# Addressing the expert weights in bytes, loading all tiles' numbers at once, and making three low halves after the first turned rows

## The chip, the cores and the metric

The kernel runs on one core of a Trainium2 chip. The time is that of the device, in microseconds, for one execution. The kernel before was timed in three runs; each kernel was also run once under the hardware profiler, and all rows below come from that execution.

## What is computed

The reference is two blocks of gated cross attention and feed-forward over x of 8 x 100 rows of 256 numbers, in float32:

```python
x = x + tanh(g_xattn[0]) * xattn0(layernorm(x), ctx)
x = x + tanh(g_ffn[0])   * ffn0(layernorm(x))
x = x + tanh(g_xattn[1]) * xattn1(layernorm(x), ctx, ctx)
x = x + tanh(g_ffn[1])   * moe(layernorm(x))
# moe: scores = softmax(x @ gate_w + gate_b), the two best of 8 experts
#      h = relu(x @ w1[e] + b1[e]);  y = h @ w2[e] + b2[e];  out = sum over the two of score * y
```

The change touches only the last line, the mixture of experts: 800 rows, each to two of E = 8 experts with hidden width DF = 1024.

## The kernel before, in words

Everything ahead of the last stage (layernorms, first block, second attention) fills the span up to about 540 us. While the second attention runs, the expert weights are brought in by POOL's queue and split in two fp16 halves, a high one (ACT) and a low one (DVE, raw value times 16 minus the high half, L1446). All eight experts stay in the on-chip tile WE, per partition `[E, 4, 2048]` fp16: m = 0, 1 are high and low of w1, m = 2, 3 of w2. One half step n = 1 to 16 makes one matrix of one expert, from expert 7 down to expert 0; LATE = 10, and steps 10 to 16 are made in the last stage by `act_step` (L1824) and `dve_step` (L1992). Semaphore s_wlo counts low halves.

The last stage sorts the 1600 (row, expert) pairs into NS = 20 tiles of 128 slots, each tile of one expert; tiles go from expert 7 to expert 0. DVE makes from the counts, for each tile, the expert number `em` and the count of low halves that must be there, `ew` = 16 - 2 e (L2087, L2088). Then the tiles are worked, and five engines run programs of their own that meet by semaphores:

- POOL (L1798 to L1819): `gather(a)` is an indirect DMA of tile a's 128 rows into one of three buffers `xg`. Three gathers go out first; then for each a it waits until tile a is turned, gathers a + 3, waits until tile a's outcome is shared out and the scatter before has landed, and scatters tile a with addition into the output. So gather(a + 4) is behind scatter(a) on POOL.
- PE: `turn(a)` (L1915) turns the gathered rows with four matmuls, high and low, two chunks; it waits for the gather, and for ACT and DVE to have copied tile a - 1. `hidden(a)` (L1929): 48 matmuls, 8 column blocks f by 2 chunks by three half products; it waits for the two copies, for s_wlo to reach the tile's number, and for tile a - 2's bias. `outcome(a)` (L1947): one matmul for the bias and 24 for the product, 256 columns each.
- ACT: `turned(a)` copies the high half, `highs(a, i)` makes ReLU and high half of half a tile, `share_out(a)` (L1861) scales the outcome.
- DVE: `turned(a)` copies the low half (L2114), `bias(a, i)` (L2116), `lows(a, i)` (L2125). It looks up the expert number of the next tile itself.

PE's order, L1971 to L1983, is: the numbers of tile 0, turn(0), turn(1), hidden(0); then for each a: `expert_in(a + 1)` (two register loads, each with a test of its bounds), turn(a + 2), hidden(a + 1), outcome(a). The weights' address is made by PE's sequencer from a register: `weights(e, m, c0, c1)` (L1926) takes WE at expert e. In hidden, the matmuls (0, 0) and (0, 1) of a block share one address, (1, 0) has another: 32 addresses a tile. In outcome (hh, 2) and (hl, 2) share one: 16 a tile, and one for the bias row.

DVE makes low halves 13 to 16 at L2107 ahead of its first `turned`; ACT makes high halves 14 to 16 at L1845, the last of which waits for a low half.

Of the kernel before, what the change touches and what calls it, by code (L numbers as in the profile page):

```python
# [7 lines left out]
F32 = mybir.dt.float32  # L8
F16 = mybir.dt.float16
I32 = mybir.dt.int32  # L10
X = mybir.AxisListType.X
XY = mybir.AxisListType.XY

P = 128
# [7 lines left out]
def flamingo(nc, x, ctx_seq, g_xattn, g_ffn,  # L22
# [18 lines left out]
    B, T, D = x.shape  # L41
# [4 lines left out]
    KC = D // P  # L46
# [7 lines left out]
    E = w1.shape[0]  # L54
    DF = w1.shape[2]
# [28 lines left out]
    with top:  # L84
# [67 lines left out]
        WE0 = 98272  # L152
# [1220 lines left out]

        WE = nc.alloc_sbuf_tensor_at("WE", [P, E, 4, KC * DF], F16, offset=WE0)
        stg = [share[:, p * KC * DF:(p + 1) * KC * DF] for p in range(2)]
        s_lb = sem("expert_low_half_begun")

# [2 lines left out]
        b2p = w1k[:, :, :, :].rearrange("p a k n -> p (a k n)")  # L1382
        s_ws = [sem(f"expert_step_staged{p}") for p in range(2)]
        s_whi = sem("expert_high_halves_made")
        s_wlo = sem("expert_low_halves_made")
        s_vz = sem("second_values_cleared")
        NWS = 2 * E
# [291 lines left out]
        xg = [in_moe(f"gathered{q}", [P, 2, D], F16) for q in range(3)]  # L1679
        idx = in_moe("slot_tokens", [P, NS], I32)  # L1680
        csl = in_moe("slot_shares", [P, NS])
        em = in_moe("tile_experts", [1, NS], I32)
        ew = in_moe("tile_weights_ready", [1, NS], I32)
        low = in_moe("low", [P, E, E])
# [77 lines left out]
        with nc.Block() as block:  # L1762
# [59 lines left out]
            @block.scalar  # L1822
            def _(act):
                def act_step(act, n):  # L1824
                    raw, loaded, count = late_raw(n)
                    act.wait_ge(loaded, count)
                    if n >= LATE + 5:

                        act.wait_ge(s_wlo, n - 3)
                    e, m = step_of(n)  # L1830
                    nc.scalar.activation(WE[:, e, 2 * m, :], raw, ACT.Copy, scale=WS).then_inc(s_whi, 1)

                for kc in range(KC):
                    act_attT(act, kc, f"o_a{kc}")
                for n in range(LATE, LATE + 3):
                    act_step(act, n)
                for i, (t0, t1) in enumerate(((0, 4), (4, NTILE))):
                    act.wait_ge(s_xn, 3 * NTILE + t1)
                    nc.scalar.activation(xhl[:, t0:t1, 0, :], xn[:, t0:t1, :], ACT.Copy).then_inc(s_xh, 1)
                act.wait_ge(s_wd, U["m_x0"] + 1)  # L1840
                nc.scalar.activation(xT32[:, 0, :], W("m_x0")[:, 0:NT], ACT.Copy).then_inc(s_xa, 1)
                act_step(act, LATE + 3)
                act.wait_ge(s_lg, 1)
                nc.scalar.activation(sc[:, :, :], lg[:, :, :], ACT.Exp).then_inc(s_ex, 1)
                for n in range(LATE + 4, LATE + 7):  # L1845
                    act_step(act, n)

                def turned(a):
                    act.wait_ge(s_tT, a + 1)
                    if a >= 2:  # L1850
                        act.wait_ge(s_hd, 2 * (a - 1))
                    nc.scalar.activation(xgT[a % 2][:, 0], TB_[0], ACT.Copy).then_inc(s_th, 1)

                def highs(a, i):
                    act.wait_ge(s_r, 2 * a + i + 1)
                    if a >= 2 and i == 0:
                        act.wait_ge(s_yd, a - 1)
                    fs = slice(i * HF, (i + 1) * HF)
                    nc.scalar.activation(hh[a % 2][:, fs, :], rr[a % 2][:, fs, :], ACT.Relu).then_inc(s_hh, 1)  # L1859

                def share_out(a):  # L1861
                    act.wait_ge(s_yd, a + 1)
                    if a >= 2:
                        act.wait_ge(s_out, 16 * (a - 1))
                    nc.scalar.activation(ysb[a % 2], YB_[a % 2], ACT.Identity, scale=csl[:, a:a + 1], bias=0.0  # L1865
                                         ).then_inc(s_ys, 1)

                turned(0)
                turned(1)
                act.wait_ge(s_cs, 1)  # L1870
                for a in range(NS):
                    for i in range(2):
                        highs(a, i)
                    if a > 0:
                        share_out(a - 1)
                    if a + 2 < NS:
                        turned(a + 2)
                share_out(NS - 1)

            @block.tensor  # L1880
            def _(pe):
# [41 lines left out]
                                                    start=(kc == 0), stop=(kc == KC - 1), skip_group_check=True)  # L1923
                    last.then_inc(s_tT, 1)

                def weights(e, m, c0, c1):  # L1926
                    return WE[:, bass.ds(e, 1), m, c0:c1].rearrange("p a n -> p (a n)")

                def hidden(a, e, ready):  # L1929
                    pe.wait_ge(s_th, a + 1)  # L1930
                    pe.wait_ge(s_tl, a + 1)
                    if a >= 2:
                        pe.wait_ge(s_r, 2 * (a - 1))

                    pe.wait_ge(s_wlo, ready)
                    for f in range(FC):
                        for kc in range(KC):
                            o0 = kc * DF + f * P
                            for m, l in ((0, 0), (0, 1), (1, 0)):
                                last = nc.tensor.matmul(WB[a % 2][:, f, :], weights(e, m, o0, o0 + P), xgT[a % 2][:, l, kc, :],  # L1940
                                                        start=(f % HF == 0 and kc == 0 and m == 0 and l == 0),
                                                        stop=(f % HF == HF - 1 and kc == KC - 1 and m == 1),
                                                        skip_group_check=True)
                        if f % HF == HF - 1:
                            last.then_inc(s_hd, 1)

                def outcome(a, e):  # L1947
                    if a >= 2:
                        pe.wait_ge(s_ys, a - 1)
                    nc.tensor.matmul(YB_[a % 2], k2, b2p[:, 0:E * D].rearrange("p (e d) -> p e d", e=E)[  # L1950
                        :, bass.ds(e, 1), :].rearrange("p a d -> p (a d)"), start=True, stop=False)
                    for f in range(FC):
                        if f % HF == 0:
                            pe.wait_ge(s_hl, 2 * a + f // HF + 1)
                        for lhs, m in ((hh, 2), (hl, 2), (hh, 3)):
                            last = nc.tensor.matmul(YB_[a % 2], lhs[a % 2][:, f, :], weights(e, m, f * D, (f + 1) * D),  # L1956
                                                    start=False, stop=(f == FC - 1 and m == 3))
                    last.then_inc(s_yd, 1)

                pe.wait_ge(s_em, 1)  # L1960
                ex, er = [], []

                def expert_in(a):
                    _, v = nc.values_load_multi_w_load_instructions(
                        em[0:1, a:a + 1], engines=[mybir.EngineType.PE], min_val=0, max_val=E - 1)
                    ex.append(v[0])
                    _, v = nc.values_load_multi_w_load_instructions(
                        ew[0:1, a:a + 1], engines=[mybir.EngineType.PE], min_val=NWS - 2 * (E - 1), max_val=NWS)
                    er.append(v[0])

                expert_in(0)  # L1971
                pe.wait_ge(s_cs, 1)
                turn(0)
                turn(1)
                hidden(0, ex[0], er[0])
                for a in range(NS):
                    if a + 1 < NS:
                        expert_in(a + 1)
                    if a + 2 < NS:
                        turn(a + 2)  # L1980
                    if a + 1 < NS:
                        hidden(a + 1, ex[a + 1], er[a + 1])
                    outcome(a, ex[a])  # L1983

            @block.vector
            def _(dve):
# [5 lines left out]
                def dve_step(dve, n):  # L1992
                    dve_step_low(dve, *step_of(n), n, late_raw(n)[0])
# [110 lines left out]
                    ex.append(v[0])  # L2104

                expert_in(0)
                for n in range(LATE + 3, LATE + 7):  # L2107
                    dve_step(dve, n)

                def turned(a):  # L2110
                    dve.wait_ge(s_tT, a + 1)
                    if a >= 2:
                        dve.wait_ge(s_hd, 2 * (a - 1))
                    nc.vector.tensor_copy(xgT[a % 2][:, 1], TB_[1]).then_inc(s_tl, 1)  # L2114
# [18 lines left out]

                turned(0)
                turned(1)
                for a in range(NS):
                    for i in range(2):
                        bias(a, i, ex[a])
                    for i in range(2):
                        lows(a, i)  # L2140
                    if a + 2 < NS:
                        turned(a + 2)
                    if a + 1 < NS:
                        expert_in(a + 1)
# [26 lines left out]
```

## Time and profile before

| | us |
|---|---|
| median of 3 runs | 744.37 |
| lowest, highest | 739.03, 749.35 |
| the profiled execution | 746.0 |
| its span, first to last instruction | 744.2 |
| PE, DVE, ACT, POOL busy in the span | 550.7, 428.9, 303.0, 150.4 |
| mean granted TensorE clock | 0.864 |

An engine's row is its busy time; "PEld" are weight loads, "PEldq" or "DVEq" what an engine's sequencer does by itself (register arithmetic, register loads, waits). The chain of work that ended last is followed back from the last instruction; "issue" in it is time in which an engine waited for nothing that the profile shows. The granted clock is given as a share of 2.4 GHz.

### The profile page before, as it was taken

The numbers are of one execution on the slowest core, as the hardware profiler recorded it, in microseconds if no ns is written. First come the engines' busy times: TensorE is split into PE (matmuls) and PEld (weight loads), VectorE is DVE, ScalarE is ACT, GpSimd is POOL, SyncE is SP. The second block draws the span as 40 slices with busy tenths as digits, with TensorE's granted clock in tenths as the row PEclk, the third lists the DMA queues.
The fourth block names the chain that finished last, engine by engine and source line by source line (L and its number), as shares of the span: only waits on it lengthen the run. The fifth ranks groups of instructions, "written<-read, shape, count | busy, mean of one in ns | idle before, by whom it ended". The sixth has DMA issues, their size and how long they took to land. (4 is left out here: it accounts for less than half of the span.)

```text
span 744.2 us, 16086 instructions
## 1 busy us (share of the span) xinstructions
PE 550.7 (74%) x5585; PEld 381.8 (51%) x5585; DVE 428.9 (58%) x892; ACT 303.0 (41%) x486; POOL 150.4 (20%) x184
## 2 busy tenths in 40 slices
PE   0463788888888876545378998997533999989985
PEld 0252346555656655422233665655332777777764
DVE  7625556765676664558626677775687433433431
ACT  1184135555555547014142677667331322222221
POOL 1200011211121111000326011022323133233222
PEclk9996759998999787857676899999655999999998
DMA  8031663444434710000355599771930012112200
GB/s 246 9 96 40 113 133 96 122 117 99 106 87 100 186 33 1 0 1 0 92 90 128 156 174 160 188 145 58 333 102 28 16 25 38 26 28 36 36 11 1
DMA packets 73249, 64.34 MB, mean 86 GB/s; under 512 B 33326, under 2 KB 65750, under 8 KB 73190
## 3 DMA queue, kind: packets, MB, share of 16 engines
q1 hardware_dynamic: 61816, 41.78, 25.1%
q0 software_dynamic: 8224, 21.06, 10.8%
q10 hardware_dynamic: 3152, 0.71, 0.5%
q8 instruction: 39, 0.64, 0.4%
q14 instruction: 18, 0.15, 0.1%
HBM read 48.59 MB, written 15.92 MB: 87 GB/s over the span
## 5 line engine op out<-in xcount | busy, mean ns | idle before, releaser
L455 PE MATMUL PS<-QS,KS 112*120 112x100 f16 (+2 forms) x896 | 92.8, 230 | 18.5 <-ACT PT L518 17.0
L455 PEld LDWEIGHTS PS<-QS,KS 112*120 112x120 f16 (+2 forms) x896 | 81.2, 143 | 44.4 <-ACT PT L518 23.3
L566 DVE CUSTOM_DVE_ANT_0 PS<-PS,maskv 100x461 f32<-100x461 f32 x128 | 80.6, 648 | 16.2 <-PE PS L424 15.2
L1940 PE MATMUL PS<-aT,WE 128*128 128x128 f16 x960 | 86.8, 229 | 1.2 <-issue 0.8
L569 DVE TENSOR_REDUCE mx<-PS 100x1 f32<-100x361 f32 x128 | 63.6, 529 | 34.2 <-PE PS L427 33.1
L1940 PEld LDWEIGHTS PS<-aT,WE 128*128 x960 | 68.7, 99 | 19.3 <-issue 3.3
L518 ACT ACTIVATE PT<-PS 120x400 f32<-120x400 f32 (+1 forms) x128 | 63.1, 502 | 32.9 <-PE PS L455 30.5
L518 ACT ACTIVATE PT<-PS,ctxb 120x400 f32<-120x400 f32 (+1 forms) x96 | 56.8, 592 | 47.2 <-PE PS L455 45.8
L2121 DVE TENSOR_TENSOR aall<-PS,b1c 128x512 f32<-128x512 f32 x40 | 27.7, 692 | 66.3 <-PE PS L1940 66.3
L424 PE MATMUL PS<-KS,QS 65*100 65x461 f16 x128 | 52.6, 416 | 11.8 <-DVE mx L566 11.5
L1859 ACT ACTIVATE hidden_high<-aall 128x512 f16<-128x512 f32 x40 | 25.2, 630 | 82.5 <-DVE aall L2121 71.6
L770 POOL TENSOR_SCALAR_AFFINE_SELECT PT<-PT 100x400 f32<-100x400 f32 x32 | 17.7, 552 | 194.6 <-ACT PT L518 194.6
L1956 PE MATMUL PS<-WE,hidden_high 128*128 x320 | 55.8, 273 | 0.0
L1816 POOL DMA_INDIRECT out_dram<-aT,slot_tokens x20 | 31.7, 1584 | 115.5 <-ACT aT L1865 108.0
L240 PE MATMUL PS<-ident,xn 128*128 128x128 f32 (+1 forms) x56 | 15.4, 425 | 47.9 <-DVE xn L228 45.1
L1602 PE MATMUL PS<-xn 128*128 128x512 f16 x142 | 48.2, 391 | 2.1 <-DVE xn L267 2.1
L427 PE MATMUL PS<-KS,QS 65*100 65x361 f16 x128 | 43.2, 364 | 6.8 <-DMA QS<-q_scratch 3.4
L1956 PE MATMUL PS<-WE,hidden_low 128*128 x160 | 43.6, 273 | 0.0
L528 ACT ACTIVATE QS<-PS 16x400 f16<-16x400 f32 (+1 forms) x32 | 25.4, 820 | 39.6 <-PE PS L436 39.5
L240 PEld LDWEIGHTS PS<-ident,xn 128*128 128x128 f32 (+1 forms) x56 | 10.4, 202 | 52.9 <-issue 47.2
L547 DVE SCALAR_TENSOR_TENSOR share<-PS,bcol,share 128x361 f16<-128x361 f32 x32 | 19.0, 594 | 30.3 <-ACT share L506 29.2
L1956 PEld LDWEIGHTS PS<-WE,hidden_high 128*128 128x128 f16 x320 | 31.2, 98 | 4.6
(300 smaller groups left out, 1076.2 us busy)
## 6 DMA issues: line engine op xcount, KB each, us to landing
share<-in_L_ffn_w_dram POOLq DMA_DIRECT2D x13, 1024.0 KB, 7.2
k_scratch<-share SPq DMA_DIRECT2D x32, 180.5 KB, 2.5
KS<-k_scratch SPq DMA_DIRECT2D x32, 180.5 KB, 3.7
KS<-k_scratch SPq DMA_DIRECT2D x64, 90.2 KB, 6.0
QS<-q_scratch SPq DMA_DIRECT2D x64, 50.0 KB, 2.5
v_scratch<-xn SPq DMA_DIRECT2D x8, 385.7 KB
values_staged<-v_scratch SPq DMA_DIRECT2D x8, 385.7 KB
WE<-in_L_ffn_w_dram POOLq DMA_DIRECT2D x2, 1024.0 KB, 8.8
```

The costliest lines, as they stand in the source:

```text
L240: last = nc.tensor.transpose(wide[n % 4][:, t0:t0 + tn], xn[0:tn, t, kc * P:(kc + 1) * P], ident[0:tn, 0:tn])
L424: nc.tensor.matmul(bank[0:T, 0:S0], QS[p][0:KROWS + 1, h, :], KS[p][0:KROWS + 1, h, :], start=True, stop=True).then_inc(s_smd, 1)
L427: nc.tensor.matmul(bank[0:T, 0:TC], QS[p][0:KROWS + 1, h, :], KS[p][0:KROWS + 1, h, 0:TC], start=True, stop=True).then_inc(s_smd, 1)
L455: last = nc.tensor.matmul(bank[0:kn, i * T:(i + 1) * T], KS[p][:, h, k0:k0 + kn], QS[p][:, h, :], start=True, stop=True)
L518: nc.scalar.activation(PT[0:kn, c, g * HG:(g + 1) * HG, :].rearrange("p h t -> p (h t)"), st_bank[t % 2][0:kn, 0:HG * T], ACT.Exp, scale=S ...
L566: nc.vector.tensor_tensor_reduce(rows, rows, maskv[:, :], 1.0, -BIG, ALU.add, ALU.max, mx[p][:, h:h + 1]).then_inc(s_smf, 1)
L569: nc.vector.tensor_reduce(mx[p][:, h:h + 1], sm_bank[h % 2][0:T, 0:TC], X, ALU.max).then_inc(s_smf, 1)
L1602: nc.tensor.matmul(misc[1], qh1[:, 0, 0:P], qh1[:, 0, 0:512], start=True, stop=True)
L1816: nc.gpsimd.indirect_dma_start(out=of[:, :], out_offset=bass.IndirectOffsetOnAxis(ap=idx[:, a:a + 1], axis=0), in_=ysb[a % 2], in_offset=N ...
L1940: last = nc.tensor.matmul(WB[a % 2][:, f, :], weights(e, m, o0, o0 + P), xgT[a % 2][:, l, kc, :], start=(f % HF == 0 and kc == 0 and m == ...
L1956: last = nc.tensor.matmul(YB_[a % 2], lhs[a % 2][:, f, :], weights(e, m, f * D, (f + 1) * D), start=False, stop=(f == FC - 1 and m == 3))
L2121: nc.vector.tensor_tensor(rr[a % 2][:, fs, :], WB[a % 2][:, fs, :], b1c[:, bass.ds(e, 1), fs].rearrange("p a f -> p (a f)").unsqueeze(2).t ...
```

## The change

- WE is allocated as bytes, and `weights` takes a slice of bytes at (16 - ready) x 8192 + a constant, read as fp16. (16 - ready) / 2 is the expert number, so PE needs only `ew`; the expert number is no longer loaded on PE. The bias row is addressed the same way.
- PE loads all 20 numbers `ew[0:1, 0:NS]` in one call ahead of turn(0), and `expert_in` is gone from its loop. DVE keeps its own.
- DVE makes low half 13 as before, and 14 to 16 behind turned(0) and turned(1), then waits for all 16. ACT makes high half 16 behind its turned(1).

```diff
-        WE = nc.alloc_sbuf_tensor_at("WE", [P, E, 4, KC * DF], F16, offset=WE0)
+        WEB = 4 * KC * DF * 2
+        WEb = nc.alloc_sbuf_tensor_at("WE", [P, E * WEB], U8, offset=WE0)
+        WE = WEb[:, :].bitcast(F16).rearrange("p (e m n) -> p e m n", e=E, m=4)
...
-                for n in range(LATE + 4, LATE + 7):
+                for n in range(LATE + 4, LATE + 6):
                     act_step(act, n)
...
                 turned(0)
                 turned(1)
+                act_step(act, LATE + 6)
                 act.wait_ge(s_cs, 1)
...
-                def weights(e, m, c0, c1):
-                    return WE[:, bass.ds(e, 1), m, c0:c1].rearrange("p a n -> p (a n)")
+                def weights(ready, m, c0, c1):
+                    return WEb[:, bass.ds((NWS - ready) * (WEB // 2) + 2 * (m * KC * DF + c0), 2 * (c1 - c0))].bitcast(F16)
...
-                    nc.tensor.matmul(YB_[a % 2], k2, b2p[:, 0:E * D].rearrange("p (e d) -> p e d", e=E)[
-                        :, bass.ds(e, 1), :].rearrange("p a d -> p (a d)"), start=True, stop=False)
+                    nc.tensor.matmul(YB_[a % 2], k2, b2p[:, bass.ds((NWS - ready) * (D // 2), D)], start=True, stop=False)
...
-                ex, er = [], []
...
-                expert_in(0)
+                _, er = nc.values_load_multi_w_load_instructions(
+                    ew[0:1, 0:NS], engines=[mybir.EngineType.PE], min_val=NWS - 2 * (E - 1), max_val=NWS)
                 pe.wait_ge(s_cs, 1)
                 turn(0)
                 turn(1)
-                hidden(0, ex[0], er[0])
+                hidden(0, er[0])
                 for a in range(NS):
-                    if a + 1 < NS:
-                        expert_in(a + 1)
                     if a + 2 < NS:
                         turn(a + 2)
                     if a + 1 < NS:
-                        hidden(a + 1, ex[a + 1], er[a + 1])
-                    outcome(a, ex[a])
+                        hidden(a + 1, er[a + 1])
+                    outcome(a, er[a])
...
                 expert_in(0)
-                for n in range(LATE + 3, LATE + 7):
-                    dve_step(dve, n)
+                dve_step(dve, LATE + 3)
...
                 turned(0)
                 turned(1)
+
+                for n in range(LATE + 4, LATE + 7):
+                    dve_step(dve, n)
+                dve.wait_ge(s_wlo, NWS)
```

## Rows read from the trace of the kernel before

**Rows 1.** The page, the chain that ended last, by line.
```profile
PE PS L1940 12%; PE PS L1956 7%; PE PS L1922 1%; DVE WE L1446 1%; PE PS L1894 1%; PE PS L240 1%; PE PS L1950 0%; PE PS L210 0%; DMA out_dram<-aT,slot_tokens 0%; DVE stats L216 0%; PE PS L211 0%; PE PS L212 0%; DVE xr L277 0%; DVE xT L2079 0
```

**Rows 2.** The chain in order of time, expert stage: start us, us, what.
```profile
572.86 0.58 PE PS L1922 x4
573.45 5.12 PE PS L1940 x48
...
585.97 0.57 issue
586.54 0.38 PE PS L1922 x4
...
599.60 2.63 PE PS L1956 x24
602.23 0.72 issue
...
610.33 0.72 issue
...
716.86 0.38 PE PS L1922 x4
...
732.50 0.48 ACT aT L1865
```

**Rows 3.** Windows: length, busy by engine, granted clock, DMA share, GB/s.
```profile
573.00:578.60 5.60, 5.60 (x54) 5.41 (x53) 1.12 (x2) 1.01 (x2) 0.00 (x0) 0.50 0.00 0
...
587.00:620.00 33.00, 30.10 (x314) 23.94 (x312) 12.71 (x21) 8.79 (x17) 10.46 (x9) 1.00 0.17 30
```

**Rows 4.** Timeline of PE around one tile: start us, us, instruction, count.
```profile
602.95 0.38 PE L1922 MATMUL PS<-wph,gathered 128*128 128x128 f16 x4 [0.72 <-issue]
603.28 4.09 PEld L1940 LDWEIGHTS PS<-aT,WE 128*128 x48
```

**Rows 5.** By source line; L1922 all tiles, others one tile: ns min/median/max, first, last start.
```profile
L1922 PE MATMUL PS<-wph,gathered x68: 216/217/218, 586.5 to 717.0; 128*128 128x128 f16 x68
...
L1940 PEldq FUSED_REGOPS  x32: 46/46/51, 595.0 to 599.1; - x32
...
L1956 PEldq FUSED_REGOPS  x16: 46/46/46, 599.3 to 601.3; - x16
...
L1964 PEldq TENSOR_LOAD <-tile_experts x1: 310/310/310, 601.4 to 601.4; - x1
L1964 PEldq FUSED_REGOPS  x1: 151/151/151, 601.8 to 601.8; - x1
...
L1967 PEldq TENSOR_LOAD <-tile_weights_ready x1: 306/306/306, 602.1 to 602.1; - x1
```

**Rows 6.** Source line L421 (attention loops), PE's sequencer.
```profile
L421 PEldq ALU_OP  x150: 32/32/36, 126.9 to 500.9; - x150
```

**Rows 7.** Timeline, share-out, scatter, gather; then source line L1799's landing.
```profile
602.27 0.47 ACT L1865 ACTIVATE aT<-PS,slot_shares 128x256 f32<-128x256 f32 x1 [1.35 <-PE PS L1956]
...
603.56 1.59 POOL L1816 DMA_INDIRECT out_dram<-aT,slot_tokens  x1 [5.29 <-ACT aT L1865]
605.46 0.98 POOL L1799 DMA_INDIRECT gathered<-rows_scratch,slot_tokens  x1 [0.30 <-issue]
...
DMA to landing us min/median/max: 2.7/2.8/4.0
```

**Rows 8.** Start of the expert tiles (source line, timeline), and the page's bias group.
```profile
L1964 PEldq TENSOR_LOAD <-tile_experts x20: 297/301/489, 561.8 to 723.6; - x20
...
565.87 1.91 ACT L1831 ACTIVATE WE<-share 128x2048 f16<-128x2048 f32 x1 [13.80 <-DVE WE L1446]
...
567.89 4.49 DVE L1446 SCALAR_TENSOR_TENSOR WE<-share,WE 128x2048 f16<-128x2048 f32 x2
...
572.29 0.42 DVE L2114 CAST aT<-PS 128x256 f16<-128x256 f32 x1
...
L2121 DVE TENSOR_TENSOR aall<-PS,b1c 128x512 f32<-128x512 f32 x40 | 27.7, 692 | 66.3 <-PE PS L1940 66.3
```

More of the change, by code:

```diff
@@ L10 @@
 I32 = mybir.dt.int32
+U8 = mybir.dt.uint8
 X = mybir.AxisListType.X
@@ L1924, in turn, with hidden @@
                     last.then_inc(s_tT, 1)
-                def weights(e, m, c0, c1):
-                    return WE[:, bass.ds(e, 1), m, c0:c1].rearrange("p a n -> p (a n)")
-                def hidden(a, e, ready):
+                def weights(ready, m, c0, c1):
+                    return WEb[:, bass.ds((NWS - ready) * (WEB // 2) + 2 * (m * KC * DF + c0), 2 * (c1 - c0))].bitcast(F16)
+                def hidden(a, ready):
                     pe.wait_ge(s_th, a + 1)
@@ L1939, in hidden @@
                             for m, l in ((0, 0), (0, 1), (1, 0)):
-                                last = nc.tensor.matmul(WB[a % 2][:, f, :], weights(e, m, o0, o0 + P), xgT[a % 2][:, l, kc, :],
+                                last = nc.tensor.matmul(WB[a % 2][:, f, :], weights(ready, m, o0, o0 + P), xgT[a % 2][:, l, kc, :],
                                                         start=(f % HF == 0 and kc == 0 and m == 0 and l == 0),
@@ L1945, in hidden, with outcome @@
                             last.then_inc(s_hd, 1)
-                def outcome(a, e):
+                def outcome(a, ready):
                     if a >= 2:
                         pe.wait_ge(s_ys, a - 1)
-                    nc.tensor.matmul(YB_[a % 2], k2, b2p[:, 0:E * D].rearrange("p (e d) -> p e d", e=E)[
-                        :, bass.ds(e, 1), :].rearrange("p a d -> p (a d)"), start=True, stop=False)
+                    nc.tensor.matmul(YB_[a % 2], k2, b2p[:, bass.ds((NWS - ready) * (D // 2), D)], start=True, stop=False)
                     for f in range(FC):
@@ L1955, in outcome @@
                         for lhs, m in ((hh, 2), (hl, 2), (hh, 3)):
-                            last = nc.tensor.matmul(YB_[a % 2], lhs[a % 2][:, f, :], weights(e, m, f * D, (f + 1) * D),
+                            last = nc.tensor.matmul(YB_[a % 2], lhs[a % 2][:, f, :], weights(ready, m, f * D, (f + 1) * D),
                                                     start=False, stop=(f == FC - 1 and m == 3))
@@ L1960, in _ @@
                 pe.wait_ge(s_em, 1)
-                ex, er = [], []
[L1963 to L1969, printed above, removed]
-                expert_in(0)
+                _, er = nc.values_load_multi_w_load_instructions(
+                    ew[0:1, 0:NS], engines=[mybir.EngineType.PE], min_val=NWS - 2 * (E - 1), max_val=NWS)
                 pe.wait_ge(s_cs, 1)
```

## The prediction, made before the changed kernel was run

> **What bounds the kernel now.** I read the page's chain first [rows 1]: it is, in the part after the attention loops, mostly matmuls of L1940 and L1956, the expert products, and "issue", time in which PE waited for nothing that the profile shows. The chain in order of time [rows 2] shows a fixed rhythm there: from the turn (L1922) at 586.54 to the one at 716.86 lie 16 tiles, so one tile takes 130.32 / 16 = 8.145 us. Each has a hole of 0.57 to 0.72 us marked "issue" before its turn. The clock is not the reason: it is at its low level (0.50, 1.2 GHz) only up to 578.6, and at the high one (1.00, 2.4 GHz) from 587 on [rows 3].
>
> Then I asked what the array itself needs. Four turn pairs (weight load and 128-column matmul, fixed address) take 0.38 us [rows 4] with the last 0.217 long [rows 5], so they follow each other every 54 ns; the 48 hidden pairs of L1940, same size, take 4.09 us in their loads, one every 85 ns [rows 4]. The difference is the address. PE's sequencer runs one FUSED_REGOPS of 46 ns per address, 32 for a tile's hidden products, from 595.0 to 599.1 [rows 5]: one every 0.13 us, whether one or two matmuls hang on it. So the hidden products wait for the sequencer. The sequencer's own sum for one tile [rows 4, 5]: hidden addresses 595.0 to 599.1 and to the outcome's first at about 599.2, outcome addresses to 601.4, then the two lookups of expert number and weight count (TENSOR_LOAD, FUSED_REGOPS, SEQ_ASSERT, twice) 601.4 to about 602.75, turn and waits to 603.2: 4.2 + 2.2 + 1.35 + 0.4 = 8.15. That is the whole cycle. PE's sequencer is the bound of this stage, not its array: the array needs 0.22 (turn) + 48 x 0.054 = 2.6 + outcome 2.63 [rows 2] and the bias matmul before it 0.1, 5.6 us in all.
>
> **The change, part by part.** I write E(a) for the end of tile a's outcome. E(0) is at 585.97, E(18) at about 732.47 [rows 2].
>
> *Lookups.* 19 pairs of lookups leave the tiles; each takes 1.35 us of the sequencer [rows 5]. Cycle by the sequencer: 8.14 - 1.35 = 6.8.
>
> *Addresses.* Each hidden and outcome address (48 a tile, and the bias row's, 49) becomes one addition. The nearest row is a lone ALU_OP of PE's sequencer, 32 ns [rows 6], against 46 now [rows 5]: 14 ns less, 49 x 0.014 = 0.7 a tile, cycle 6.1. Bounds: nothing gained (it stays a 46 ns fused operation) and, as no shorter operation stands in these rows, 14 ns. I take 14, since the new text has one addition where the old one indexes in elements of two bytes. The first address of a tile also multiplies; that is one operation of about 46 ns as now.
>
> *What is late next.* With 6.1 the next chain must be looked at, and it is POOL's [rows 7]. After the outcome's end at 602.23 ACT shares out at 602.27, POOL's scatter starts at 603.56, the gather queued behind it at 605.46, and it lands 2.8 us later, 608.26: E(a) + 6.03. That gather(a+4) is used by turn(a+4), which follows outcome a+1. Today turn(a+4) stands 8.145 + 0.68 = 8.8 after E(a), 2.7 us of cover. After the change E(a+1) is at E(a) + 6.1, and the sequencer, which runs ahead of the array during the outcome (its addresses end at 601.3, the matmuls at 602.23), wants the turn some 0.6 before that, at + 5.5. It would find the rows missing for 0.6 us. So turn(a+4) comes at E(a) + 6.13. From a turn to the end of the outcome that follows it (a hidden product lies between) is 610.33 - 602.95 = 7.4 [rows 2, 4], on average 8.145 - 0.68 = 7.46; with 32 faster hidden addresses 7.46 - 0.45 = 7.0 (the outcome goes by the array). Two tiles take 6.13 + 7.0 = 13.1, one 6.6 us. DVE's two biases, two low halves and a copy (0.69 for a bias, the low halves taken as long, 0.42 the copy [rows 8]: 3.2 and its own lookup of about 1) fit in 6.6; POOL's scatter and gather (1.59 and 0.98 [rows 7]) too.
>
> *The start.* All 20 numbers are read and tested ahead of the first turn. One test (FUSED_REGOPS, SEQ_ASSERT) takes from 601.8 to the next load at 602.1, 0.29 us [rows 5]. Load at 561.8, 0.49 long [rows 8]; 561.8 + 0.55 + 20 x 0.29 = 568.2 for turn(0), where it was at 565.9 after its gather. But DVE no longer makes three low halves before its copy of turn(0) (two of them are the 4.49 us from 567.89 [rows 8], so one is 2.25). Turn(0) 0.6, copy and way back 0.57 (572.29 to 572.86), turn(1) at 569.4 in place of 572.86 [rows 2, 8]: hidden(0) 3.5 earlier, at 569.7, ending at 574.9 (5.12 at the low clock [rows 2]), hidden(1) to about 579.1. In that time DVE makes its three low halves, 570.5 + 3 x 2.25 = 577.2, then bias, bias, low of tile 0, three times 0.69 with ACT's high half beside the second [rows 8]: 579.3. So the moved halves are hidden behind hidden(0) and hidden(1) but for 0.2 us; without that cover they would cost their 6.75. ACT's moved high half (1.91 [rows 8]) runs from about 570.5 to 572.4, and DVE needs it at 575. Outcome(0) ends at 579.3 + 2.8 = 582.1: E(0) is 3.9 earlier. Bounds of this part: the single load of 20 numbers is not in the trace. At 0.3 it is as above; as 20 loads of 0.36 each it adds 6.8 us, and the gain of 3.9 turns into a loss of 2.9.
>
> **The sum.** From E(0) to E(18) now 732.47 - 585.97 = 146.5. After: 17 tiles at 6.6 and the last, which has no turn, at 6.1: 118.3. Gain 28.2 + 3.9 = 32.1 us. What follows E(18) (scatter 18, its landing, the last scatter) stays. The profiled execution took 746.0 us (span 744.2): 713.9. The median of the runs shown, 744.37, is 1.6 lower; I say 712. A difference of 2%, 15 us, is about what a measurement can tell here (the three runs before lie 10 us apart).
>
> The Trainium skill, "TensorE: Matmul & The Clock Gate", section "Back-to-back issue gap", gives about 81 ns as the sustained distance of weight load and matmul pairs of 128 columns. The turn's four pairs at 54 ns [rows 4] do not agree, but four are no long run. By that rule the hidden products could hardly get faster and the sum would be that of the second rival below.
>
> **Rivals.**
> *The gather is no limit.* If the rows land earlier than E(a) + 6.0, or the sequencer's lead is smaller than I think, the cycle is the sequencer's 6.1 throughout: 18 x 6.1 = 109.8 in place of 118.3, 8.5 us more gained, 704. For it: landing is between 2.7 and 4.0 [rows 7]. Against: scatter and gather starts repeat to 0.1 us in tile after tile.
> *Hidden products stay at 85 ns a pair.* Either the address stays a 46 ns operation, or the array cannot take different weights every 54 ns for 48 pairs running. Then turn to end stays 7.46, the cycle is (6.13 + 7.46) / 2 = 6.8, with the last at 6.8: 122.4, gain 24.1 + 3.9 = 28.0, 716. With the dear load at the start (6.8 more) it is 723.
> *Slower: addresses that don't fuse.* The new address is written with a subtraction, a multiplication and an addition; today's three register outputs are packed into one operation. If the packing or the reuse of the product is lost, a second lone operation costs its 32 ns and the gap of about 80 ns that stands between sequencer operations in the lookup (151 ns from 601.8, next at 602.0 [rows 5]). That is 110 - 14 = 96 ns on each of 49 addresses, 4.7 a tile against 1.35 saved: 19 x 3.35 = 64 us slower, 808. It decides from 1.35 / 49 = 28 ns per address on. Against: the elements are bytes, so no scaling is left, and the product is the same for a whole tile.
>
> **How the numbers follow.** Forecast (gather-bound, 712) 0.50; no gather limit 0.15; hidden products unchanged, with or without a dear start, 0.25; addresses longer by about the break-even, or the lookups' time showing again as another wait, within 2%, 0.05; slower 0.05. The first three are all faster by over 2%: 0.90. The range takes in 704 and 723 and 2 us on each side for the spread of medians: 702 to 725.
>
> **What would show it.** In the changed trace: no TENSOR_LOAD of PE's sequencer after 570; ALU_OP of about 32 ns in place of FUSED_REGOPS in the hidden lines, their matmuls every 76 ns or less; turn(1) at 569 to 570; a cycle of 6.6 in which long and short tiles alternate, with PE waiting before the turn for the gathered rows; DVE's last three low halves under PE's first hidden products. I am wrong if the cycle stays above 7.5, if the sequencer shows two or more operations per address, or if turn(1) comes after 573.

## The result, and the profile after

Median of five runs 716.31 us (714.41 to 726.25) against 743.69 (five runs, 738.92 to 749.35) of the kernel before on the same chip: 27.4 us less. The ratio on record, from all runs and not from the medians, is 0.967 (95% interval 0.963 to 0.971). The forecast was 712, the range 702 to 725.

The profiled execution of the changed kernel is the slowest of its five, the 726.25 one. It was late already when the expert stage began: slot_tokens, the row numbers that the gathers use, was written at 568.63, in the other kernels between 554 and 566. So I count from slot_tokens on, in every kernel. Three stretches make up the stage:

| from slot_tokens | before | after | forecast gain | measured gain |
|---|---|---|---|---|
| to E(0), the end of outcome 0 | 24.04 | 21.34 | 3.9 | 2.7 |
| E(0) to E(18) | 146.50 | 122.77 | 28.2 | 23.7 |
| E(18) to the end | 11.78 | 11.78 | 0 | 0 |

The stage gained 26.4 us, the medians 27.4. The two need not agree, since the medians hold what is ahead of the stage as well. The page's chain of the changed kernel, by line, answers to [rows 1]: hidden products (now L1946) fell from 12% to 7% of the span, and there is a landing in it that was not there.

```profile
PE PS L1946 7%; PE PS L1961 6%; DMA gathered<-rows_scratch,slot_tokens 2%; POOL out_dram L1821 1%; PE PS L1900 1%; PE PS L1928 1%; DVE WE L1450 1%; PE PS L241 1%; PE PS L1956 0%; PE PS L211 0%; DMA out_dram<-aT,slot_tokens 0%; PE PS L213 0%; PE PS L212 0%; DVE stats L217 0%; DVE xr L278 0%
```

The chain in order of time (start, us, what), against [rows 2]. L1928 is the turn, L1961 the outcome, L1450 a low half:

```profile
568.63 0.19 DVE slot_tokens L2085
...
575.93 0.60 PE PS L1928 x4
...
586.37 0.70 DVE hidden_low L2123
...
587.19 2.78 PE PS L1961 x24
589.97 0.22 PE PS L1928 x4
590.19 3.28 PE PS L1946 x48
...
596.29 0.22 PE PS L1928 x4
...
603.25 0.48 ACT aT L1870
...
604.54 1.59 POOL out_dram L1821
...
606.44 4.39 DMA gathered<-rows_scratch,slot_tokens
610.88 0.40 PE PS L1928 x4
611.28 3.88 PE PS L1946 x48
```

Three things are to be seen. The hole of some 0.6 to 0.8 us before each turn is gone: a turn starts where an outcome ends (589.97, 596.29). The hidden products take 3.3 us in one tile and 3.9 in another; the cycles alternate (6.32, 6.92, 6.35 us from E(0) on). And the fourth is 8.42 long: the chain leaves PE at 603.25, passes share-out and scatter, and comes back only when a gather has landed, 4.39 us after its start. The same happens at two more places:

```profile
640.97 4.15 DMA gathered<-rows_scratch,slot_tokens
...
675.15 4.35 DMA gathered<-rows_scratch,slot_tokens
```

By source line, PE's sequencer in the stretch from 592 to 597, and the load of the 20 numbers (ns min/median/max, first and last start), against [rows 5]:

```profile
L1946 PEldq ALU_OP  x16: 32/32/32, 592.0 to 596.9; - x16
L1946 PEldq MOVE  x1: 29/29/29, 596.3 to 596.3; - x1
L1946 PEldq FUSED_REGOPS  x1: 51/51/51, 596.3 to 596.3; - x1
```

```profile
L1966 PEldq FUSED_REGOPS  x20: 146/146/165, 570.1 to 575.5; - x20
L1966 PEldq SEQ_ASSERT  x20: 18/18/28, 570.3 to 575.7; - x20
L1966 PEldq TENSOR_LOAD <-tile_weights_ready x1: 1544/1544/1544, 568.5 to 568.5; - x1
```

L1946 again, in the stretch from 589.2 to 589.45, one tile earlier:

```profile
L1946 PEldq MOVE  x1: 29/29/29, 589.3 to 589.3; - x1
```

Each address is one ALU_OP of 32 ns; only the first of a tile is fused, with a MOVE before it. The sequencer began the addresses of one tile at 589.3, 0.7 us before the outcome ahead of it ended (589.97), and those of the next at 596.3, just as that outcome ended (596.29). Behind the one load of L1966 no register load follows. The load took 1.54 us, and its tests last to 575.7. The granted clock, against [rows 3], is 1.00 (2.4 GHz) through the tiles:

```profile
592.00:700.00 108.00, 105.64 (x1198) 91.79 (x1197) 48.82 (x79) 31.73 (x62) 40.53 (x32) 1.00 0.21 37
```

### The profile page after: what moved, and what is told of

It reads as the page before. It is cut to its first block and busy times, and to the rows that moved or that the text cites. A ratio compares the mean times of both kernels' runs of the same rounds, so it can differ in the third digit from the quotient of the medians.

```text
span 724.5 us, 16028 instructions
## 1 busy us (share of the span) xinstructions
PE 542.1 (75%) x5585; PEld 385.3 (53%) x5585; DVE 428.5 (59%) x892; ACT 301.5 (42%) x486; POOL 149.0 (21%) x184
## 5 line engine op out<-in xcount | busy, mean ns | idle before, releaser
L456 PE MATMUL PS<-QS,KS 112*120 112x100 f16 (+2 forms) x896 | 94.6, 233 | 18.6 <-ACT PT L519 17.0
L456 PEld LDWEIGHTS PS<-QS,KS 112*120 112x120 f16 (+2 forms) x896 | 83.5, 146 | 45.7 <-ACT PT L519 23.7
L1946 PE MATMUL PS<-aT,WE 128*128 128x128 f16 x960 | 74.7, 222 | 0.4
L1946 PEld LDWEIGHTS PS<-aT,WE 128*128 x960 | 66.0, 99 | 8.0 <-issue 1.8
L1961 PE MATMUL PS<-WE,hidden_high 128*128 x320 | 55.6, 273 | 1.3 <-DVE hidden_low L2123 1.3
L2114 DVE TENSOR_TENSOR aall<-PS,b1c 128x512 f32<-128x512 f32 x40 | 27.4, 690 | 48.3 <-PE PS L1946 44.5
L1606 PE MATMUL PS<-xn 128*128 128x512 f16 x142 | 50.2, 405 | 2.1 <-DVE xn L268 2.1
L1961 PE MATMUL PS<-WE,hidden_low 128*128 x160 | 43.6, 273 | 0.0
L1961 PEld LDWEIGHTS PS<-WE,hidden_high 128*128 128x128 f16 x320 | 31.2, 98 | 5.2 <-issue 1.5
```

Source lines behind the costliest of these rows:

```text
L456: last = nc.tensor.matmul(bank[0:kn, i * T:(i + 1) * T], KS[p][:, h, k0:k0 + kn], QS[p][:, h, :], start=True, stop=True)
L1606: nc.tensor.matmul(misc[1], qh1[:, 0, 0:P], qh1[:, 0, 0:512], start=True, stop=True)
L1946: last = nc.tensor.matmul(WB[a % 2][:, f, :], weights(ready, m, o0, o0 + P), xgT[a % 2][:, l, kc, :], start=(f % HF == 0 and kc == 0 and m ...
L2114: nc.vector.tensor_tensor(rr[a % 2][:, fs, :], WB[a % 2][:, fs, :], b1c[:, bass.ds(e, 1), fs].rearrange("p a f -> p (a f)").unsqueeze(2).t ...
```

## The experiments

All were timed beside runs of the kernel before, whose medians were 743.67 to 743.96. A median and its stage can differ by some us in what they gain (e3: 7.1 by the medians, 4.4 in the stage; e8: 52.4 and 48.1), since the part ahead of the stage varies from run to run; the terms below are read from the stage. The intervals of e2 and e9 overlap that of the changed kernel, so for these two the stage alone tells them apart from it. Start is from slot_tokens to E(0), tiles from E(0) to E(18) and a cycle's mean; the tail was 11.78 or 11.79 in all but the two near 1020 us (16.3 and 16.4).

| kernel | median us | ratio [95%] | start | tiles (mean) |
|---|---|---|---|---|
| before | 743.7 | 1 | 24.04 | 146.50 (8.14) |
| after | 716.31 | 0.967 [0.963, 0.971] | 21.34 | 122.77 (6.82) |
| e1_bytes_only | 732.66 | 0.986 [0.982, 0.990] | 23.52 | 137.94 (7.66) |
| e2_elements | 721.15 | 0.968 [0.963, 0.974] | 21.35 | 126.96 (7.05) |
| e3_moves_only | 736.6 | 0.991 [0.987, 0.995] | 19.58 | 146.53 (8.14) |
| e4_four_gathers | 708.58 | 0.955 [0.951, 0.959] | 21.33 | 114.62 (6.37) |
| e5_no_tests | 1023.6 | 1.372 [1.365, 1.379] | 19.74 | 424.40 (23.6) |
| e6_halves_later | 712.14 | 0.957 [0.952, 0.962] | 19.83 | 120.97 (6.72) |
| e7_all_three | 1019.22 | 1.372 [1.365, 1.378] | 18.18 | 424.54 (23.6) |
| e8_fixed_expert | 691.6 | 0.930 [0.924, 0.935] | 21.31 | 101.16 (5.62) |
| e9_bounds_stated | 713.31 | 0.959 [0.953, 0.964] | 20.93 | 121.44 (6.75) |
| e10_best | 704.89 | 0.949 [0.944, 0.954] | 17.84 | 114.41 (6.36) |

### e1_bytes_only: the byte addresses alone

The kernel before, with both lookups kept in every tile:

```diff
-                    return WE[:, bass.ds(e, 1), m, c0:c1].rearrange("p a n -> p (a n)")
+                    return WEb[:, bass.ds((NWS - ready) * (WEB // 2) + 2 * (m * KC * DF + c0), 2 * (c1 - c0))].bitcast(F16)
```

> The kernel before with byte addresses alone; PE still loads and tests both numbers in each tile. If PE's sequencer bounds the stage: 49 addresses of 32 to 34 ns in place of 46 make a tile 0.6 to 0.7 us shorter, the cycle goes from 8.14 to 7.5, the rows of each gather are there in time at that cycle, and the kernel comes to about 732 us. If the array bounds the hidden products at 85 ns a pair: cycle 8.14, 744 us.

Measured 732.66 us, the cycle 7.66 in place of 8.14. The sequencer's work in hidden, by source line, for all 20 tiles:

```profile
L1943 PEldq ALU_OP  x620: 32/32/36, 569.1 to 716.1; - x155
...
L1943 PEldq FUSED_REGOPS  x20: 62/63/76, 569.0 to 712.3; - x20
```

The addresses became single additions here too (620 = 20 x 31), but 0.48 us a tile over 48 addresses is 10 ns for each, not 14. Part of the difference is that the first of a tile now takes a MOVE (29 ns) and a longer fused operation.

### e2_elements: the changed kernel with addresses in fp16 elements

The tile is allocated as fp16 elements (`WEh`), and:

```diff
-                    return WEb[:, bass.ds((NWS - ready) * (WEB // 2) + 2 * (m * KC * DF + c0), 2 * (c1 - c0))].bitcast(F16)
+                    return WEh[:, bass.ds((NWS - ready) * (WEB // 4) + m * KC * DF + c0, c1 - c0)]
```

> The changed kernel with the weights addressed in fp16 elements again (three operations fused, 46 ns), all else as changed. If the gathered rows limit the cycle, only the hidden addresses between a turn and the end of its outcome count, half of them in each cycle: 32 x 0.012 / 2 = 0.2 us a tile, +4 us, 720. If the cycle is the sequencer's alone: 49 x 0.012 = 0.6 a tile, +11 us, 727.

Measured 721.15 us. By source line, hidden, all tiles:

```profile
L1946 PEldq FUSED_REGOPS  x640: 46/46/85, 571.5 to 707.9; - x160
```

All 640 addresses are 46 ns operations again, as in [rows 5], and most tiles are alike at 6.9 to 7.0 us. At that cycle the gather is in time for most of them, and the sequencer is the bound by itself. Against the 6.37 of the four-buffer kernel below, where it also is, 49 byte addresses are worth 0.55 to 0.6 us a tile, 12 ns each.

### e3_moves_only: the moved halves alone

The kernel before, with the moved halves of the change and nothing else of it (on ACT high half 16 behind its turned(1) as well):

```diff
-                for n in range(LATE + 3, LATE + 7):
-                    dve_step(dve, n)
+                dve_step(dve, LATE + 3)
...
+                for n in range(LATE + 4, LATE + 7):
+                    dve_step(dve, n)
+                dve.wait_ge(s_wlo, NWS)
```

> The kernel before with the three low halves and ACT's high half moved behind the first turned rows, nothing else. My theory: turn(1) comes at about 569 in place of 572.9, DVE's chain of three low halves and the first biases ends at about 579.5, outcome(0) ends near 581.5 to 582, 4 us earlier, cycle 8.14: 740 us. Rival: the halves were hidden anyway or only change places with a later wait of the same length: 744 us. Together with the next-to-last term this says how much the 20 tests ahead of the first turn take back.

Measured 736.6 us (ten runs). The start is 4.46 us shorter and the tiles are untouched (146.53). Its chain:

```profile
566.84 0.61 PE PS L1923 x4
567.45 4.00 PE PS L1941 x48
```

turn(1) (566.84) leads straight into hidden(0), with nothing of DVE between. In the changed kernel, with the same edit, the start is 2.7 us shorter: the load and the tests of all numbers take back 1.76 us.

### e4_four_gathers: a fourth gather buffer

The changed kernel with a fourth buffer `xg`; gather(a + 4) leaves POOL before scatter(a) instead of behind it:

```diff
...
-                    if a + 3 < NS:
+                    if a + 4 < NS:
                         pool.wait_ge(s_tT, a + 1)
-                        gather(a + 3)
+                        gather(a + 4)
...
```

> The changed kernel with four buffers for gathered rows: gather(a + 4) is issued ahead of scatter(a), one tile earlier than now, into a fourth buffer of 1 KB per partition. If the gathered rows limit the changed kernel: no wait for them is left, the cycle falls from 6.85 to the sequencer's 6.2 and all tiles are alike but for code loads, 18 x 0.65 = 11.7 us less, 705. If they don't: cycle 6.85, 716.

Measured 708.58 us. One tile of the chain:

```profile
628.10 0.22 PE PS L1929 x4
628.33 3.26 PE PS L1947 x48
631.59 0.19 PE PS L1957
631.78 2.62 PE PS L1962 x24
```

The alternation is gone, all 18 cycles lie between 6.26 and 6.44, and no gather stands in the chain from 578 to 692. So the gather behind the scatter was what made every second tile long and the late landings visible: 122.77 - 114.62 = 8.15 us. What is left, 6.37, is the sequencer's cycle, for which I had said 6.1.

### e5_no_tests: 18 of the numbers loaded without stated bounds

The changed kernel. 18 of the 20 tests ahead of turn(0) were to go, some 5 us of the sequencer's work. From tile 2 on hidden waits for all 16 low halves by a constant.

```diff
-                    ew[0:1, 0:NS], engines=[mybir.EngineType.PE], min_val=NWS - 2 * (E - 1), max_val=NWS)
+                    ew[0:1, 0:2], engines=[mybir.EngineType.PE], min_val=NWS - 2 * (E - 1), max_val=NWS)
+                _, later = nc.values_load_multi_w_load_instructions(
+                    ew[0:1, 2:NS], engines=[mybir.EngineType.PE],
+                    skip_runtime_bounds_check_because="DVE makes them from counts of experts, 2 to 16")
```

> The changed kernel with the test of bounds kept for the first two tiles' numbers alone; the other 18 are loaded without one, and from tile 2 on PE waits for all 16 low halves in place of the tile's number (they are all made by then). In the changed kernel PE loads 1.54 us and tests 20 times 0.29, so turn(0) comes 3.3 us after its rows have landed. My theory: this is the part of the start that the change gives back; turn(0) comes 3.3 us earlier, DVE's chain behind it too, outcome(0) ends 3.3 us earlier: 713. Rival: DVE, busy with low half 13 until just before, or the gathers hold the start anyway: under 1 us, 716.

This missed altogether: 1023.6 us. By source line, the second load, and the sequencer in hidden:

```profile
L1968 PEldq TENSOR_LOAD <-tile_weights_ready x1: 4281/4281/4281, 566.7 to 566.7; - x1
```

```profile
L1946 PEldq SEQ_ASSERT  x864: 18/18/18, 584.9 to 1001.0; - x173
L1946 PEldq ALU_OP  x638: 32/32/36, 572.7 to 1001.1; - x160
L1946 PEldq FUSED_REGOPS  x578: 62/168/224, 572.6 to 1000.8; - x193
```

864 = 18 x 48: every matmul of the 18 tiles now has a test of its address, of 168 + 18 ns with the gaps between. With the outcome's it is 72 a tile, and (23.6 - 6.4) / 72 = 0.24 us for each. The array has the same products to do. Its granted clock was down at 0.50 to 0.53 in the tiles (windows 600 to 700 and 900 to 1000), but even at half speed its part of a tile, 5.63 us in e8, comes to an estimated 11.3, half of the 23.6. So the sequencer sets the time here, and the stage is three times as long. By itself this doesn't show where the bound of the changed kernel lies, since enough work added to any engine would show; that rests on the runs that took work away (e1, e8). It is also my slower rival, by another door: more operations per address.

### e6_halves_later: two low halves deferred

The changed kernel; low halves 15 and 16 are made behind the lows of tiles 1 and 2:

```diff
-                for n in range(LATE + 4, LATE + 7):
-                    dve_step(dve, n)
-                dve.wait_ge(s_wlo, NWS)
+                dve_step(dve, LATE + 4)
+                dve.wait_ge(s_wlo, LATE + 4)
...
+                    if a in (1, 2):
+                        dve_step(dve, LATE + 4 + a)
```

> The changed kernel with low halves 15 and 16 (expert 0, first needed by tile 7 at the earliest) moved once more on DVE, behind the low halves of tiles 1 and 2. In the changed trace outcome(0) waits from 585.7 to 587.2 for the first hidden low half, which is behind three expert halves on DVE. Theory: that wait of 1.5 us goes, DVE's slack of some 2 us per tile takes the two halves of 2.25: 1.5 us less, 715. Rival: the halves then delay the biases of tiles 2 and 3 by as much: no change, or up to 2 us more, 716 to 718.

Measured 712.14 us, the start 1.51 shorter. The tiles are 1.8 shorter as well, which the edit doesn't explain: this run's slow landings in the tiles took 3.3, 3.8 and 4.2 us, those of the changed kernel 4.39, 4.15 and 4.35. The chain goes from hidden(1) into outcome(0) with the bias matmul alone between (L1956), where the changed kernel stands for 1.34 us, up to 587.19:

```profile
571.56 2.72 PE PS L1946 x48
574.28 0.20 PE PS L1956
574.49 2.62 PE PS L1961 x24
```

### e7_all_three: four buffers, e5's loads and e6's halves together

> Four gather buffers, no tests from the third number on, and the two halves later, together on the changed kernel. If the three are independent: cycle 6.37, start 3.3 + 1.5 us shorter than with four gathers alone (708.6): 704. If the start's two edits hit the same wait: 706.

Measured 1019.22 us, by the same tests as e5. It says no more than e5, except that the start, where those tests hardly count, falls to 18.18.

### e8_fixed_expert: no address arithmetic at all

Four buffers, and all weights of w1 and w2 taken from expert 7 at a fixed address. This leaves out the choice of the expert in the products:

```diff
-                    return WEb[:, bass.ds((NWS - ready) * (WEB // 2) + 2 * (m * KC * DF + c0), 2 * (c1 - c0))].bitcast(F16)
+                    return WE[:, 7, m, c0:c1]
```

> The changed kernel with four gather buffers and every tile's weights taken from expert 7 at a fixed address: it leaves out the choice of the expert for w1 and w2 (the biases are still chosen), so no address operation stands between the matmuls. If PE's sequencer is still the bound with four buffers (cycle 6.37): hidden pairs follow each other every 55 to 57 ns, the cycle falls to the array's 5.7 to 5.8, 18 x 0.6 = 11 us less than four gathers alone, 698. If 48 pairs running cannot go below about 81 ns (the page's figure; the sum by it is 6.9 a tile) or below 75: cycle 6.4 or more, 708 or more.

Measured 691.6 us. One tile of its chain:

```profile
606.65 2.62 PE PS L1962 x24
609.27 0.22 PE PS L1929 x4
609.50 2.68 PE PS L1947 x48
612.17 0.11 PE PS L1957
```

The cycle is 5.63 in tile after tile, where the prediction had counted 5.6 for the array. The hidden pairs follow each other every 2.68 / 48 = 55.8 ns. So the array's floor is 0.74 us a tile below what one addition per address allows. That measurement refutes the 81 ns a pair that the prediction took from the Trainium skill, "TensorE: Matmul & The Clock Gate", section "Back-to-back issue gap". The same page of the Trainium skill, section "Wait — 56ns, not 53.3ns?", gives 55.6 ns from start to start for back-to-back matmuls of 128 columns at the high clock, and the run agrees.

### e9_bounds_stated: 4 numbers tested, 16 with bounds stated but no test

```diff
-                    ew[0:1, 0:NS], engines=[mybir.EngineType.PE], min_val=NWS - 2 * (E - 1), max_val=NWS)
+                    ew[0:1, 0:4], engines=[mybir.EngineType.PE], min_val=NWS - 2 * (E - 1), max_val=NWS)
+                _, later = nc.values_load_multi_w_load_instructions(
+                    ew[0:1, 4:NS], engines=[mybir.EngineType.PE],
+                    min_val=NWS - 2 * (E - 1), max_val=NWS,
+                    skip_runtime_bounds_check_because="DVE makes them from counts of experts, 2 to 16")
```

From tile 2 on hidden waits for all 16 low halves by a constant.

> The changed kernel with the first four numbers loaded and tested, the other 16 loaded from a start that is a multiple of four numbers, their bounds stated but not tested; from tile 2 on PE waits for all 16 low halves. What it tells apart from the run whose 18 numbers had no stated bounds: if there the missing bounds put a test at nearly every weight address (1296 SEQ_ASSERT between the matmuls), none stands here and the cycle is 6.8 again; if the two loads or the constant wait were the cause, it stays at 24 us a tile. Start: loads of 0.5 and 1.2, four tests 1.2, so turn(0) follows its gather's landing at 4.0 us after the slot numbers in place of 7.3: 3.3 us less than the changed kernel, 713. If the load from number 4 costs 240 ns a number, as the one from number 2 did (4.28 us for 18), turn(0) comes at 5.7 and the kernel takes 715.

Measured 713.31 us. The loads, by source line:

```profile
L1966 PEldq TENSOR_LOAD <-tile_weights_ready x1: 516/516/516, 560.2 to 560.2; - x1
```

```profile
L1968 PEldq TENSOR_LOAD <-tile_weights_ready x1: 1127/1127/1127, 562.0 to 562.0; - x1
```

turn(0) came 3.95 us after slot_tokens in place of 7.30, and no test came back in the tiles (mean 6.75, with 620 additions in hidden as after). But E(0) is only 0.4 us earlier. The chain shows the first half of the reason: turn(1) now waited for its gather (started at 562.79, landed 3.91 later), so that DVE's last low half of tile 0 was only 2.1 us earlier against slot_tokens. The windows show the second half (stretch, length, busy by engine PE, PEld, DVE, ACT, POOL, granted clock, DMA share, GB/s):

```profile
571.40:575.00 3.60, 3.60 (x53) 3.18 (x50) 3.45 (x3) 0.00 (x0) 0.00 (x0) 1.00 0.02 5
575.20:576.80 1.60, 0.16 (x1) 0.00 (x0) 1.44 (x4) 1.44 (x3) 0.00 (x0) 1.00 0.00 0
576.80:581.30 4.50, 4.45 (x28) 3.41 (x28) 3.34 (x6) 1.23 (x3) 0.00 (x0) 0.62 0.00 0
```

PE stood 1.5 us for DVE's low half, and outcome(0) behind it ran mostly at the low clock, 4.46 us in place of 2.78. The changed kernel stood nearly as long (1.34 us, up to 587.19) and kept its 2.4 GHz:

```profile
587.20:590.00 2.80, 2.80 (x28) 2.53 (x29) 2.70 (x6) 1.23 (x2) 0.00 (x0) 1.00 0.00 0
```

So 713.31 fits what was expected, but not by the sum that I had written.

### e10_best: four buffers, e9's loads, e6's halves

As the three diffs above, with the wait for low halves a constant 14 for tiles 2 to 6 and 16 behind.

> Four gather buffers, the two loads with four tests, and low halves 15 and 16 behind tiles 1 and 2, together. Four buffers gave cycle 6.37 (708.6), the later halves 1.5 us of the start, and the tests should give 3.3: 704 if they add, 706 if the start's two edits hit the same wait. If the untested numbers still bring tests at the addresses: about 1020.

Measured 704.89 us. Its chain at the start:

```profile
567.61 0.61 PE PS L1929 x4
568.22 4.14 PE PS L1947 x48
...
572.58 3.54 PE PS L1947 x48
...
576.33 2.62 PE PS L1962 x24
```

PE goes from turn(1) through outcome(0) without a stop. The stage takes 17.84 + 114.41 + 11.78 = 144.0 us against 155.9 of the changed kernel, 11.9 less; the intervals of the two ratios do not touch. Of these 3.5 are at the start and 8.4 in the tiles. The tiles' part is e4's. The start's is more than 0.4 (e9) and 1.5 (e6) together: without the idle of e9 outcome(0) ran at 2.4 GHz (2.62 us), so that the 2.1 us by which e9's low halves had come earlier counted in full, and 2.1 + 1.5 is about the 3.5.

## Why the prediction was right, and where it was off

**The bound: right.** PE's sequencer set the stage before. The changed kernel and e1 took work off it and gained, e5 added work to it and came out 280 us above the kernel before, and e8 took its addresses away and met the array's 5.63 against the forecast's 5.6. In the changed kernel the sequencer and the gathers share the bound.

**The lookups: right.** e1 and e4 differ in the tiles by the lookups (and the bias row's address), apart from the gathers, by which neither is held: 7.66 - 6.37 = 1.29 us a tile, forecast 1.35.

**The addresses: right in kind, too large.** 32 ns operations as forecast, but 10 ns (e1) to 12 ns (e2 against e4) gained per address, not 14, and MOVE plus FUSED_REGOPS of 80 ns at a tile's first. The sequencer's cycle is 6.37, not 6.1.

**What is late next: right.** The rule was gather(a + 4) behind scatter(a), landed at E(a) + 6.03, turn at + 6.13, two tiles 13.1. Measured: E(0) at 589.97, gather(4) from 593.30 with a landing of 2.7, so at about 596.0, E(0) + 6.0 as forecast; turn(4) at 596.29, + 6.3; two tiles 6.32 + 6.92 = 13.24. That the sum is so near is in part luck: the first term came out too short and the second too long. I had written that the wait would show as PE's idle time before the turn; it doesn't. The array is still at the outcome when the rows land, and only the sequencer waits: it loses its lead of 0.7 us (addresses begun at 589.3 in one tile, at 596.3 in the next), and the hidden products behind take 3.9 in place of 3.3. e4 removes it.

**The landing: the term that failed.** I took 2.8 us for every landing, though [rows 7] has a maximum of 4.0 (a gather of the start; in the tiles before the slowest took 3.9). Before, such a one was covered by 2.7 us; after, there is no cover, and each costs up to its excess of 1.3 to 1.6 us. At 6.35 and 6.9 in turn, with 6.34 and 6.23 for the last two, 18 cycles are 8 x 13.25 + 12.57 = 118.6, all but the 118.3 forecast; the measured 122.77 is 4.2 more. The three late landings fall into cycles of 8.42, 7.26 and 7.53, and their excesses add to 4.5, so the 4.2 is theirs in the main; a gather that started 0.35 us late and a landing of 3.1 make two more cycles 0.3 to 0.4 longer. In each of their windows lies one packet of queue q8 (instruction), as here from 606.4 to 611 (queue: packets, MB, share; then issue and landing):

```profile
q0 software_dynamic: 192, 0.26, 34.9%
q8 instruction: 1, 0.02, 1.3%
...
gathered<-rows_scratch,slot_tokens POOLq DMA_INDIRECT x1, 4.4
```

A gather from 612.78 on, without such a packet up to its landing, took 2.7. By the records these 16 KB packets come every 8 to 9 us, and the three late gathers have one 1.7 to 2.4 us behind their start. But with one at 0.74 us a gather took 2.9, and in e4 two with one at 2.2 to 2.3 took 2.8. Over all twelve traces, without each kernel's first four gathers, there are 145 gathers with a known landing. All 25 that took 3.3 us or more have such a packet 0.2 to 2.4 us behind their start, 13 more have one there and took 3.2 or less, and none of the 89 without one from 0.6 before to 2.8 behind took over 3.0. Among the first four, which follow each other closely, landings of 3.6 to 4.0 stand without a packet. So the coincidence is shown, the cause only argued: no run took the packets away. How many gathers of a run meet one is luck.

**The start: 3.9 forecast, 2.7 found.** The step that failed is the single load of 20 numbers: 1.54 us, where I took 0.55 (0.3 to 6.8 more had been the bounds). The 20 tests took 5.6 (570.1 to 575.7), 5.8 as forecast. turn(0) was 7.3 behind slot_tokens, about 1.0 late, and DVE's low halves began so much later. turn(1) stands at 577.12; put on the time scale of the kernel before, whose slot_tokens is at 561.93, that is 570.4, just behind the 569 to 570 that I had named and well before the 573 that would have shown me wrong. DVE's chain of low halves took what I had said: 578.08 to 587.07, 9.0 us against 6.75 + 2.07 = 8.8. The cover for them was shorter than I thought, since hidden(1), at the high clock and with its addresses begun 1.2 us ahead of it (581.5), ran in 2.9 us, not in 4.2; the timeline of PE shows it, and the wait:

```profile
577.50 5.19 PE L1946 MATMUL PS<-aT,WE 128*128 128x128 f16 x48
...
582.75 2.89 PE L1946 MATMUL PS<-aT,WE 128*128 128x128 f16 x48
...
587.19 0.27 PE L1961 MATMUL PS<-WE,hidden_high 128*128 x1 [1.34 <-DVE hidden_low L2123]
```

So where I had all but 0.2 us of the moved halves hidden, 1.5 us of them showed (e6).

**The rivals.** *No gather limit* (704) is what e4 built, and it gave 708.6, since the sequencer's own cycle is 6.37. *Hidden products stay at 85 ns a pair* forecast 716, the very time measured, and is wrong all the same: they take 3.3 us or 69 ns a pair where the rows are in time, 2.9 or 60 ns where the sequencer has a lead. A time that fits is no evidence for its mechanism. *Addresses that don't fuse* did not come, but e5 shows that the mechanism is real. Its price was read wrongly: the gap between sequencer operations in the lookup is 0.06 us (a FUSED_REGOPS from 601.82 to 601.97, the next operation at 602.03), not 0.08.

**The sum.** The stage gained 26.4 where 32.1 was forecast: 4.2 late landings, 1.2 the start, 0.3 the two-tile cycle. The median is 4.3 us above the forecast, and even the lowest of the five runs (714.41) is above it.

## What to carry to other kernels

Where matmuls are addressed by a register, count the sequencer's operations per weight load before looking at the array: here 49 addresses a tile, with the lookups, were the bound before, and again once the gathers were out of the way (e4), where the array's floor lay another 0.74 us below (e8). When a change shortens a cycle, recompute each chain that used to have cover, and with its slowest instance, not its median. Values that a loop needs can be loaded ahead in one instruction, but their tests stand in front of the first use, and the 18 values loaded here without stated bounds were tested at every use (e5).

## What the hardware showed that was not expected

- A register load's time doesn't go by its count alone: 1 number mostly 0.30 us, whichever it is [rows 8], 2 numbers 0.73, 4 in 0.52, 16 in 1.13, 20 in 1.54, but 18 starting at the third number 4.28 us (e5). The others started at the first or the fifth number. What makes that one long was not tried.
- An idle of PE of 1.5 us was followed by a fall of the granted clock to 1.2 GHz in one kernel (e9, 1.7 us lost in the next 24 matmuls), one of 1.3 us by none in another (after). Both had had hidden(0) and hidden(1) ahead of it, in 5.2 and 2.9 us in the one that kept its clock, in 4.3 and 3.7 in the one that lost it. What decides was not tried.
- In the tiles, indirect gathers that are otherwise alike land mostly in 2.7 to 2.9 us, and now and then in 3.3 to 4.4, each of these with a packet of the instruction queue close behind its start.
